# Expert blocks of a two-expert MoE kernel: loads that turn the block on the way in, instead of TensorE transposes

## What is computed

```python
x = x + 0.5 * ffn(layernorm(x), ...)
x = x + attention(layernorm(x), ...)
x = x + 0.5 * ffn(layernorm(x), ...)
```

```python
logits = x @ gate_w                       # 8 experts
top_v, top_i = top_k(logits, 2)
combine[token, top_i] = softmax(top_v)
g = einsum('th,ehi->tei', x, Wg)          # expert width 352
u = einsum('th,ehi->tei', x, Wu)
d = einsum('tei,eih->teh', silu(g) * u, Wd)
out = einsum('te,teh->th', combine, d) + shared_ffn(x)
```

## Time and profile before

| what | value |
|---|---|
| time, median of 3 runs | 1507.25 us (1504.07 to 1507.92) |
| profiled execution, span from the first to the last instruction | 1500.4 us |
| median of the runs less that span | 6.9 us |
| first expert phase, first load to last scatter | about 248.7 to 512 us |
| second expert phase | about 1190.5 to 1454.5 us |
| busy share of the span: PE, DVE, ACT, POOL | 72%, 74%, 46%, 58% |

### The profile page before, as it was taken

One profiled execution on the slowest core, in us unless ns is written; L12 is line 12 of the kernel. 1 busy time (PEld: TensorE's weight loads), 2 busy tenths in 40 slices (PEclk: granted clock), 3 DMA queues, 4 the chain that ended last, 5 costly groups with the idle time before them and its releaser, 6 DMA issues.

```text
span 1500.4 us, 34500 instructions
## 1 busy us (share of the span) xinstructions
PE 1082.9 (72%) x9786; PEld 847.5 (56%) x9787; DVE 1112.3 (74%) x2822; ACT 685.5 (46%) x1497; POOL 873.0 (58%) x902
## 2 busy tenths in 40 slices
PE   3667764999999457666676767676775499999950
PEld 2555554888888334444444444454544388888850
DVE  6676655777777557899889898989886467777747
ACT  4344441555555233454444444445342155555535
POOL 4566663677777533566656565646553467777750
PEclk9687775999999877899888887979787699999985
DMA  9211113222222210000000000000000322222229
GB/s 270 44 43 43 38 40 68 69 74 75 76 74 77 60 29 14 23 30 29 30 23 28 23 29 27 28 14 14 14 15 15 72 66 75 75 73 75 71 66 302
DMA packets 119701, 86.75 MB, mean 58 GB/s; under 512 B 13717, under 2 KB 111439, under 8 KB 119662
## 3 DMA queue, kind: packets, MB, share of 16 engines
q1 hardware_dynamic: 102254, 52.41, 13.7%
q0 software_dynamic: 17408, 33.87, 6.4%
HBM read 45.01 MB, written 43.30 MB: 59 GB/s over the span
## 4 chain that ended last, share of the span: by engine, by line
POOL 27%; issue 26%; PE 14%; DVE 12%; DVEq 9%; ACT 5%; POOLq 3%; DMA 2%; SPq 2%; ACTq 0%
POOL expert_results L428 13%; POOL routed_rows L420 9%; PE PSUM L802 5%; POOL carrier L426 5%; DVEq L1002 2%; DVE prod L1203 2%; DVEq L1228 2%; PE PSUM L804 2%; DVE space L1206 2%; PE PSUM L717 2%; DVEq L1057 2%; DVE ya L972 1%; PE PSUM L710 1%; PE PSUM L712 1%; PE PSUM L711 1%
## 5 line engine op out<-in xcount | busy, mean ns | idle before, releaser
L420 POOL DMA_INDIRECT routed_rows<-row,idx x256 | 271.0, 1059 | 94.8 <-issue 94.8
L428 POOL DMA_INDIRECT expert_results<-ey,eidx x288 | 284.9, 989 | 69.8 <-issue 67.8
L802 PE MATMUL PSUM<-space,upto 128*128 128x320 f32 (+1 forms) x384 | 195.0, 630 | 57.2 <-DVE prod L1203 54.8
L588 ACT ACTIVATE esil<-PSUM 128x768 f32<-128x768 f32 x144 | 116.7, 810 | 258.7 <-PE PSUM L712 258.7
L972 DVE SCALAR_TENSOR_TENSOR ehT<-eh,ehT 128x768 f16<-128x768 f32 x144 | 138.0, 958 | 118.3 <-ACT ehT L593 118.1
L442 POOL TENSOR_TENSOR space<-qk,val 128x1152 f32<-128x1152 f32 x64 | 148.3, 2328 | 87.2 <-DVE qk L1196 87.0
L710 PE MATMUL PSUM<-WD,ehT 128*128 x864 | 153.3, 219 | 7.1 <-DVE ehT L972 7.1
L802 PEld LDWEIGHTS PSUM<-space,upto 128*128 128x128 f32 x384 | 85.8, 238 | 124.8 <-issue 104.2
L711 PE MATMUL PSUM<-WD,ehT 128*128 x864 | 153.0, 219 | 0.0
L712 PE MATMUL PSUM<-WD,ehT 128*128 x864 | 152.9, 219 | 0.0
L1206 DVE TENSOR_REDUCE space<-prod 128x144 f32<-128x1152 f32 x64 | 141.3, 2208 | 5.8
(11 more groups left out here) (195 smaller groups left out, 3005.0 us busy)
## 6 DMA issues: line engine op xcount, KB each, us to landing
xe<-routed_rows SPq DMA_DIRECT2D x144, 130.0 KB
space<-expert_results SPq DMA_DIRECT2D x64, 256.0 KB, 3.8
expert_results<-ey,eidx POOLq DMA_INDIRECT x288
X<-in_L_attn_x_dram SPq DMA_DIRECT2D x16, 256.0 KB, 5.2
routed_rows<-row,idx POOLq DMA_INDIRECT x256, 2.4
out_dram<-X SPq DMA_DIRECT2D x16, 256.0 KB, 4.4
routed_rows<-pad_rows SPq DMA_DIRECT2D x24, 130.0 KB
space<-in_L_ffn_Wg_dram SPq DMA_DIRECT2D x1, 1408.0 KB, 9.1
```

The source lines that it names most:

```text
L420: pool.indirect_dma_start(routed, bass.IndirectOffsetOnAxis(ap=idx[u][:, k, j:j + 1], axis=0), row[u][:, j, :], None).then_inc(s_scattered ...
L428: pool.indirect_dma_start(result, bass.IndirectOffsetOnAxis(ap=eidx[u][:, h:h + 1], axis=0), ey[u][:, h, :], None, bounds_check=K * T - 1, ...
L802: mm = pe.matmul(PKV[:, lo:hi], upto[:, :], kv[:, q, a, lo:hi], start=True, stop=(a == 0))
```

## The change

Each block is brought in already turned. SP now starts three transfers for a block: two that transpose while they move, each with 256 rows x 128 float16 columns of `routed_rows` (the high parts, then the low parts) straight into `eT[v][:, a, :]`, and a third with the two marks of each row, 8 bytes x 256 rows, into a small tile `marks[v]`. There are four buffers (`XT` = 4) of `eT` and `marks` where there were two of `xe` and `eT`. SP waits for the gate-up products and the places of block n-4 before it fills their buffers again.

PE's four transposes in each block go, and with them the bank `PE_T`; DVE's copy of 128 x 512 values goes. `block_gate_up` waits for the two turning transfers of its own block, and DVE's `block_in`, which now only works out the places, waits for the marks. The loops of SP and DVE are unrolled by four instead of two; PE's was already.

```diff
-        xe = [sb(f"xe{u}", [P, HALVES, WORDS]) for u in range(2)]
-        eT = [sb(f"eT{u}", [P, 2, BLK], F16) for u in range(2)]
+        marks = [sb(f"marks{u}", [P, HALVES, 2]) for u in range(XT)]
+        eT = [sb(f"eT{u}", [P, 2, BLK], F16) for u in range(XT)]
...
-                    wait(sp, s_block_T, n - 1)
-                    wait(sp, s_block_places, n - 1)
-                    at = sp.value_load(row_i[0:1, bass.ds(m, 1)], min_val=0, max_val=ROWS - BLK)
-                    sp.dma_start(xe[u][:, :, :], routed[bass.ds(at, BLK), :].rearrange("(h p) w -> p h w", p=P)
-                                 ).then_inc(s_block_rows[u], 16)
+                wait(sp, s_block_products, n - (XT - 1))
+                wait(sp, s_block_places, n - (XT - 1))
+                at = sp.value_load(row_i[0:1, bass.ds(m, 1)], min_val=0, max_val=ROWS - BLK)
+                for a in range(2):
+                    sp.dma_start(eT[v][:, a, :], turned_rows[bass.ds(at, BLK), a * D:(a + 1) * D], transpose=True
+                                 ).then_inc(s_block_rows[v], 16)
+                sp.dma_start(marks[v][:, :, :], routed[bass.ds(at, BLK), D:WORDS].rearrange("(h p) w -> p h w", p=P)
+                             ).then_inc(s_block_marks[v], 16)
...
-            def block_transposes(n, u):
-
-                pe.wait_ge(s_block_rows[u], (n - u) * 8 + 16)
-                wait(pe, s_block_T, n)
-                for part in range(2):
-                    for h in range(HALVES):
-                        at = part * BLK + h * P
-                        mm = pe.transpose(PE_T[:, at:at + P],
-                                          xe[u][:, h, part * D // 2:(part + 1) * D // 2].bitcast(F16), ident[:, :])
-                mm.then_inc(s_block_turned, 1)
...
-            def block_gate_up(n, u, e):
-                pe.wait_ge(s_block_T, n + 1)
+            def block_gate_up(n, u, v, e):
+                pe.wait_ge(s_block_rows[v], (n - v) * (32 // XT) + 32)
...
-                    if ahead:
-                        block_transposes(n + 1, 1 - u)
-                    block_gate_up(n, u, e)
+                    block_gate_up(n, v % 2, v, e)
...
-            def block_in(n, u, m):
-                dve.wait_ge(s_block_turned, n + 1)
-                dve.tensor_copy(eT[u][:, :, :], PE_T[:, 0:2 * BLK].rearrange("p (a t) -> p a t", a=2)).then_inc(s_block_T, 1)
-
-                dve.tensor_scalar(second[:, u, :], xe[u][:, :, WORDS - 1], eb[:, bass.ds(m, 1)], float(T),
+            def block_in(n, u, v, m):
+                dve.wait_ge(s_block_marks[v], (n - v) * (16 // XT) + 16)
+                dve.tensor_scalar(second[:, u, :], marks[v][:, :, 1], eb[:, bass.ds(m, 1)], float(T),
                                   ALU.not_equal, ALU.mult)
                 dve.drain()
-                dve.tensor_tensor(places[:, cols(m, HALVES)], second[:, u, :], xe[u][:, :, WORDS - 2], ALU.add).then_inc(s_block_places, 1)
+                dve.tensor_tensor(places[:, cols(m, HALVES)], second[:, u, :], marks[v][:, :, 0], ALU.add).then_inc(s_block_places, 1)
```

More of the change, by code:

```diff
@@ L43 @@
 WORDS = 130
+XT = 4
 NOTOK = float(1 << 20)
@@ L215, in macaron @@
         s_row_ends, s_padded = sem("s_row_ends"), sem("s_padded")
-        s_block_rows = [sem("s_block_rows0"), sem("s_block_rows1")]
-        s_block_turned, s_block_T, s_block_products, s_block_silu, s_block_hidden, s_block_high, s_block_low, s_block_out, s_block_results, s_block_places = (
-            sem("s_block_turned"), sem("s_block_T"), sem("s_block_products"), sem("s_block_silu"), sem("s_block_hidden"), sem("s_block_high"), sem("s_block_low"),
+        s_block_rows = [sem(f"s_block_rows{v}") for v in range(XT)]
+        s_block_marks = [sem(f"s_block_marks{v}") for v in range(XT)]
+        s_block_products, s_block_silu, s_block_hidden, s_block_high, s_block_low, s_block_out, s_block_results, s_block_places = (
+            sem("s_block_products"), sem("s_block_silu"), sem("s_block_hidden"), sem("s_block_high"), sem("s_block_low"),
             sem("s_block_out"), sem("s_block_results"), sem("s_block_places"))
@@ L320, in pads, with load_block, load_blocks @@
                 sp.wait_ge(s_padded, 16 * (E * (f + 2)))
-            def load_block(f):
-                def step(n, u):
-                    m = n - f * NBLK
-                    wait(sp, s_block_T, n - 1)
-                    wait(sp, s_block_places, n - 1)
-                    at = sp.value_load(row_i[0:1, bass.ds(m, 1)], min_val=0, max_val=ROWS - BLK)
-                    sp.dma_start(xe[u][:, :, :], routed[bass.ds(at, BLK), :].rearrange("(h p) w -> p h w", p=P)
-                                 ).then_inc(s_block_rows[u], 16)
-                return step
+            turned_rows = routed.bitcast(F16)
+            def load_block(f, n, v):
+                m = n - f * NBLK
+                wait(sp, s_block_products, n - (XT - 1))
[6 more added lines that the diff above has]
+                             ).then_inc(s_block_marks[v], 16)
+            def load_blocks(f):
+                n0 = f * NBLK
+                for v in range(XT):
+                    load_block(f, n0 + v, v)
+                with sp.Fori(0, (NBLK - 2 * XT) // XT) as i:
+                    for v in range(XT):
+                        load_block(f, i * XT + (n0 + XT + v), v)
+                for v in range(XT):
+                    load_block(f, n0 + NBLK - XT + v, v)
             def results(g, k):
@@ L353, in _ @@
                 phase_end(sp, 2 * f + 1)
[L354 removed]
+                load_blocks(f)
                 phase_end(sp, 2 * f + 2)
@@ L848, in block_gate_up @@
                         at = 1536 * u + o + c * BLK
-                        mm = product(PSUM[:, at:at + BLK], w, [eT[u][:, 0, :], eT[u][:, 1, :]])
+                        mm = product(PSUM[:, at:at + BLK], w, [eT[v][:, 0, :], eT[v][:, 1, :]])
                 mm.then_inc(s_block_products, 1)
@@ L864, in experts, with step @@
                 n0, n1 = f * NBLK, (f + 1) * NBLK
-                def step(n, u, e, e_down=None, ahead=True):
-                    if ahead:
-                        block_transposes(n + 1, 1 - u)
-                    block_gate_up(n, u, e)
+                def step(n, v, e, e_down=None):
+                    block_gate_up(n, v % 2, v, e)
                     if e_down is not None:
-                        block_down(n - 2, u, e_down)
+                        block_down(n - 2, v % 2, e_down)
                 e = experts_of(0, 2)
-                block_transposes(n0, 0)
                 step(n0, 0, e[0])
@@ L879, in experts @@
                     for b in range(4):
-                        step(i * 4 + (n0 + 2 + b), b % 2, e[b + 2], e[b])
+                        step(i * 4 + (n0 + 2 + b), (2 + b) % XT, e[b + 2], e[b])
                 e = experts_of(NBLK - 4, 4)
-                step(n1 - 2, 0, e[2], e[0])
-                step(n1 - 1, 1, e[3], e[1], ahead=False)
+                step(n1 - 2, (NBLK - 2) % XT, e[2], e[0])
+                step(n1 - 1, (NBLK - 1) % XT, e[3], e[1])
                 block_down(n1 - 2, 0, e[2])
@@ L1149, in experts, with step @@
                 n0, n1 = f * NBLK, (f + 1) * NBLK
-                def step(n, u, ahead=True):
+                def step(n, v, ahead=True):
+                    u = v % 2
                     if ahead:
-                        block_in(n + 1, 1 - u, n + 1 - n0)
+                        block_in(n + 1, 1 - u, (v + 1) % XT, n + 1 - n0)
                     block_low(n - 1, 1 - u)
                     block_mult(n, u)
-                block_in(n0, 0, 0)
-                block_in(n0 + 1, 1, 1)
+                block_in(n0, 0, 0, 0)
+                block_in(n0 + 1, 1, 1, 1)
                 block_mult(n0, 0)
-                block_in(n0 + 2, 0, 2)
+                block_in(n0 + 2, 0, 2, 2)
                 block_low(n0, 0)
                 block_mult(n0 + 1, 1)
[L1163 to L1167, removed]
+                with dve.Fori(0, (NBLK - 4) // XT) as i:
+                    for b in range(XT):
+                        step(i * XT + (n0 + 2 + b), (2 + b) % XT)
+                step(n1 - 2, (NBLK - 2) % XT)
+                step(n1 - 1, (NBLK - 1) % XT, ahead=False)
                 block_low(n1 - 1, 1)
```

1 line of the change is left out of this document (removed).

## The result

| | median | runs |
|---|---|---|
| before | 1505.66 us | 4 (1499.57 to 1507.92) |
| changed kernel | 1594.38 us | 4 (1591.68 to 1597.80) |

The changed kernel is slower: ratio 1.0608, 95% interval 1.057 to 1.0645, that is +88.7 us where 38 to 41 us less were forecast. The time lies inside the range of the prediction, two thirds of the way up, and on the other side of its forecast. The rival "The turning issue holds SP" is what happened.

What follows compares the result with a forecast made beforehand. PE was taken to set the pace in both expert phases. Transposes 30.8, late loads 7.2 and starts 2.8 give 40.8 us off: span 1459.6, plus 6.9 is 1466.4, say 1467 us; range 1458 to 1660.

Steps and rivals of the forecast that it cites:

- The turning issue holds SP: Rival on SP's queue: three issues per block make SP the limit, from 1520 up to 1870 us; chance 0.37.
- I take 0.378: Assumed time in us that each turning transfer's issue holds SP's queue, taken from the plain issue; SP's round then 2.3 us.
- three bounds: Candidate turning-issue times on SP's queue: plain issue 0.378 us, POOL's indirect issue 0.99, queue held until landing 2.24.
- What PE gains: PE, expert phases: 30.8 us from transposes, 7.2 from late loads, 2.8 from phase starts, 40.8 us off in all.
- The starts: First load to first gate product in each expert phase: 4.19 us becomes 2.8, saving 1.4 per phase, 2.8 in all.
- Points (a) to (d): No other engine takes over: POOL needs 2.73 us, DVE waits anyway, ring keeps 0.24 and 0.38, output buffer 1.2 spare.
- the ring: Dependency circle PE - ACT - DVE - PE: narrowed but not closed, 0.24 us and 0.38 us spare remaining.
- The wait for marks: DVE's new wait, ahead of its low part and multiplication: costs nothing as long as SP keeps up.
- The DMA engines: Not the limit: 1.9 of 3.17 us per block, unless a turning packet takes some 0.07 us.
- scatters: Rival: delayed output scatters or POOL bind, so the gain falls to 20 us, time 1488 us; chance 0.10.
- no change: Rival: SP's round is 3.40 to 3.46 us by accident, or PE's time goes into the narrow ring; chance 0.06.
- T: Time one turning transfer's issue holds SP's queue; up to 0.81 us free, SP's round being 1.25 + 0.30 + 2T.

## Why the prediction was wrong

**The step that failed** is "I take 0.378, because line 329 has the same queue, the same source and the same 256 rows". The turning issue holds the queue for 1.144 to 1.146 us at 128, 256 and 512 rows alike. It was above the 0.94 us from which, by the prediction, the rival decides, and by that rival's own sum SP's round would be 1.25 + 0.30 + 2 x 1.144 = 3.84 us and the time 1507 + 140 x (3.84 - 3.44) = 1563 us; measured were a round of 4.04 and 1594. The register work around three issues was 0.2 us dearer than my 0.84 + 0.30; with 4.04 the same sum gives 1591. A price that no row showed was set at the lowest of three bounds, where the prediction's own rows had the other kind of special transfer, POOL's, at 0.99; that one was the nearer. The version with plain transfers shows that this step alone turned the sign: with the assumed price on the queue, the kernel is faster than before.

On the issue's price the Trainium skill ("DMA: Bandwidth & Descriptors", "Why a DMA increments its semaphore by 16 and not by 1") gives 631 cycles for small tiles against 512 for a plain copy, a factor of 1.23; here it is 1144 against 378 ns, 3.0, and the measurement decides. The Trainium skill ("Advanced Engine Details and Errata", "X-Bar Transpose (TRN2)") says that turning transfers are as fast as regular ones. For the movement itself the traces agree: from 300 to 340 us a packet of q1 takes 0.015 us of an engine in the changed kernel and 0.254 x 16 x 40 / 9866 = 0.016 with plain transfers. The landing, which has the issue in it, is 2.4 us in the median, against 2.05 for a plain transfer of the same 64 KB at that version's first start.

**What PE gains** was right in its pace and too high in its sum. Between heads a block takes 2.97 us with plain transfers, to the digit. Of the earlier trace rows together I made four blocks of 4 x 2.97 + 0.84 = 12.72 us; they take 13.27. The table has the medians of the distance from one block's first gate weight load to the next one's, for the four steps around PE's loop head (first phase, 262 to 500 us before and 262 to 490 us with plain transfers):

| | ahead of the head | across the head | next | last | four blocks |
|---|---|---|---|---|---|
| before | 3.43 | 4.03 | 3.16 | 3.19 | 13.81 |
| plain transfers | 2.97 | 4.26 | 2.93 | 3.11 | 13.27 |

Of the 0.54 us gained, 0.23 is the late load of `xe`: at the end of the step ahead of the head, the distance from the last down weight load to the first gate one, with the transposes in it, is 0.51 us instead of 0.28. That leaves 0.3 us for the transposes, where 4 x 0.22 = 0.88 were forecast. The head's "issue" of 0.84 was read as a cost on top of the transposes, while they ran inside a stretch in which the queue was busy anyway. The step across the head even became 0.23 us longer without them, and the last step gained 0.08 instead of 0.22. Why these two steps lose what they lose no row names. So "140 x 0.22 = 30.8 us lie squarely on the path" should have been some 35 x 0.3 = 11 us. Counted from their first loads, the two expert phases are 10.7 and 12.4 us shorter in that version, of which the runs' medians show 16.5.

**The starts** gave nothing to speak of in the changed kernel: from the first load's issue to the first gate product it takes 4.22 and 3.85 us in the two phases, against 4.31 and 3.99 before (the prediction's 4.19 was read 0.2 too long: in the timeline the product starts at 1194.55). Two turning issues, 2.86 us with what lies between them in the first phase, take what the transposes and the copy gave. With plain transfers the starts take 3.18 and 2.70, which is 2.4 us of the forecast 2.8.

**Points (a) to (d)** held. With one turning transfer POOL waits for ACT in 15 of some 60 blocks (270 to 470 us) where it was 63 of 67, about once for each of PE's loop heads: it keeps up, with little to spare between them. No row of that stretch shows PE waiting in the ring, and ACT waits once for a scatter, 0.7 us. **The wait for marks** held too, in the sense that it was tied to SP keeping up: it does not, and DVE waits in all 68 blocks from 270 to 550 us. **The DMA engines** as forecast are no limit. The rivals of scatters and of no change did not happen.

**The chances** were 0.37 for what happened. That the time fell inside the range is owed to the room left for this rival, not to the forecast. The error is not in the mechanism, which was there with its place, its threshold and a bound, but in the value for T and in giving it more weight than its evidence had. The sum for PE, had SP kept up, would have been too high as well, by some 20 us.

## What to carry to other kernels

Count the issues on a queue before the bytes: a transfer of a new kind can hold its queue several times longer than a plain one (here three times) while the DMA engines are mostly idle, and buffers ahead don't help a queue that never waits. If the price is for each issue, lay the data out so that one issue carries what two did. And before taking work off an engine, look at whether its queue was busy with something else at that moment: here work that ran inside such a stretch was free, and removing it gained nothing there.

## What the hardware showed unexpectedly

- A turning transfer's issue on SP's queue lasts 1.144 us for 128 x 128 and for 256 x 128 float16 values, and 1.146 us for 512 x 128; a plain one lasts 0.37 to 0.43 us. Its landing goes from 2.4 us (256 rows) to 3.0 (512).
- A moving operand read at every second float16 column costs 0.113 us for 256 columns in place of 0.109.
- Loading expert numbers for six blocks and branching back on PE's queue leaves 1.26 to 1.29 us (medians) between weight loads, with or without four transposes inside, and 1.14 where the other three blocks have transposes too.
- On some chips the kernel before took 1.11 times as long, and the versions without transposes in most blocks 1.14 to 1.15 times, so the order of two versions one per cent apart was the other way round.
